# A search step's soundness flags: from a VectorE chain to eighteen GpSimd columns summed by TensorE

## The reference

```
for s in range(2):
    logits = (Xa @ W1) @ W2 @ (Xa @ W3).T
    # per row: keep the largest logits until their softmax mass reaches 0.9
    A  = softmax(where(keep, logits, -inf))
    Xf = Rf @ Xf;  Xb = Rb @ Xb;  Xa = A @ Xa
    Z  = Z + Xf @ U1[s] + Xb @ U2[s] + Xa @ U3[s]
out = x + layernorm(X + Z) * gamma + beta
```

## Time and profile before

| | us |
|---|---|
| median of 3 runs | 2169.99 (2163.16 to 2171.1) |
| profiled execution, its own time | 2169.9 |
| its span, first to last instruction | 2168.2 |

### The profile page before, as it was taken

The page is one execution under the profiler, slowest core; times in us unless marked ns, Lnnn a source line. Parts: engine busy times, 40 slices in busy tenths (PEclk is TensorE's granted clock), DMA queues, the critical chain, the costliest instruction groups (busy, mean ns, idle before and its releaser), DMA issues. The chain is left out here.

```text
span 2168.2 us, 32420 instructions
## 1 busy us (share of the span) xinstructions
PE 1883.3 (87%) x9866; PEld 1252.5 (58%) x9866; DVE 1912.8 (88%) x6117; ACT 1678.5 (77%) x1740; POOL 711.0 (33%) x1392
## 2 busy tenths in 40 slices
PE   3999765999999999999864999989998999999992
PEld 2566433666666666666642656565655566565662
DVE  7788889988899998889748899999999999999995
ACT  5444256999999999999626899989999898989840
POOL 2000043444334444434504333333333333333324
PEclk9999987999999999999986999999999999999996
DMA  7788330111111111111125010101010010101023
GB/s 262 295 317 312 114 130 20 34 56 55 51 55 55 35 54 55 51 55 56 34 75 207 1 45 23 45 23 45 23 36 32 24 44 23 45 23 45 22 94 121
DMA packets 65725, 167.61 MB, mean 77 GB/s; under 512 B 7037, under 2 KB 45307, under 8 KB 61947
## 3 DMA queue, kind: packets, MB, share of 16 engines
q1 hardware_dynamic: 65530, 165.43, 22.0%
HBM read 117.95 MB, written 47.45 MB: 76 GB/s over the span
## 5 line engine op out<-in xcount | busy, mean ns | idle before, releaser
L1468 PE MATMUL banks<-xa,pt 128*128 128x256 f32 x2704 | 644.2, 390 | 14.5 <-ACT pt L968 13.7
L1468 PEld LDWEIGHTS banks<-xa,pt 128*128 128x128 f32 x2704 | 507.0, 194 | 158.9 <-issue 71.3
L939 ACT ACTIVATE junk_a<-pb_all,minus_t 128x3327 f16<-128x3327 f32 x150 | 461.0, 3073 | 98.9 <-POOLq L862 96.4
L944 ACT ACTIVATE junk_a<-pb_all,minus_t 128x3327 f16<-128x3327 f32 x150 | 460.6, 3071 | 4.1
L1519 PE MATMUL banks<-region,at 128*128 128x512 f16 x2028 | 455.7, 380 | 0.0
L847 POOL TENSOR_SCALAR over<-over,points 128x1 f32<-128x1 f32 x150 | 97.1, 647 | 761.0 <-ACT junk_a L944 761.0
L1519 PEld LDWEIGHTS banks<-region,at 128*128 128x128 f16 x2028 | 196.4, 98 | 217.7 <-issue 1.3
L1394 PE MATMUL banks<-keys,qs 64*128 64x512 f32 (+1 forms) x816 | 190.1, 565 | 100.7 <-DMA qs<-q_d 31.0
L1260 DVE TENSOR_SCALAR_CACHE_REDUCE pb_all<-banks 128x1024 f32<-128x1024 f32 x260 | 209.2, 848 | 31.1 <-PE banks L1394 22.6
L1122 DVE MAX8 junk_v<-below 128x8 f32<-128x208 f32 (+1 forms) x624 | 222.4, 432 | 2.2
L968 ACT ACTIVATE pt<-banks 128x896 f32<-128x896 f32 x208 | 171.1, 859 | 63.6 <-PE banks L1460 63.4
(11 more groups left out here) (221 smaller groups left out, 2738.5 us busy)
## 6 DMA issues: line engine op xcount, KB each, us to landing
at<-adjT_d SPq DMA_DIRECT2D x52, 832.0 KB, 4.9
region<-in_adj_dram SPq DMA_DIRECT2D x25, 1663.5 KB, 7.9
adjT_d<-at SPq DMA_DIRECT2D x26, 832.0 KB, 3.9
fb_d<-fb_sb SPq DMA_DIRECT2D x26, 256.0 KB, 2.0
region<-fb_d SPq DMA_DIRECT2D x2, 3328.0 KB, 17.7
y_d<-y_sb SPq DMA_DIRECT2D x50, 128.0 KB, 1.7
x_d<-pb_all SPq DMA_DIRECT2D x1, 3328.0 KB, 10.4
qs<-q_d SPq DMA_DIRECT2D x104, 32.0 KB, 4.2
```

Of the source, the lines that this page charges most:

```text
L939: nc.scalar.activation(junk_a[:, 0:w], pb[u][:, 0:w], ACT.Relu, scale=sign, bias=t, accum_out=over[u][:, 0:1])\
L944: nc.scalar.activation(junk_a[:, 0:w], pb[u][:, 0:w], ACT.Sign, scale=sign, bias=t, accum_out=over[u][:, 1:2])\
L1468: last = nc.tensor.matmul(bank[4][:, 0:D], pt[sl][:, t * P:(t + 1) * P], xa[:, t0 + t, :], start=(t0 + t == 0), stop=(t0 + t == T - 1))
```

## The change

In step one only, VectorE no longer computes the flags. It signals `ranked` after the scan that makes `rank`. GpSimd gets a new function `flags(i)`, placed after level 0 of the tile two ahead and ahead of low_sub: it writes 18 columns, one for each segment and two for `took` and `left_max`, and signals `unsettled`. TensorE's first flag sum becomes a product of a column of ones with the 18 columns, and VectorE's `answer` takes the maximum of the 18 sums. VectorE writes `rest` in place where it wrote `same` and `rank`, because GpSimd still reads these.

```
...
                def flags(i):
                    by_segment = [v[:, 0:8 * G].rearrange("p (g e) -> p g e", e=8)[:, :, 7] for v in (cand, same, rank)]
                    pool.wait_ge(S("ranked"), i.t + 1)
                    after(pool, "any_psum", i, per=LOOKS)
                    ch.add(nc.gpsimd.tensor_scalar(signs_of[:, G:G + 1], took[:, :], 0.0, None, ALU.is_le))
                    ch.add(nc.gpsimd.tensor_scalar(signs_of[:, G + 1:G + 2], left_max[:, :], 0.0, None, ALU.is_le))
                    ch.add(nc.gpsimd.tensor_scalar(signs_of[:, 0:G], by_segment[2], ties[:, :], None, ALU.is_lt))
                    ch.link(nc.gpsimd.tensor_scalar(full[:, 0:G], by_segment[0], left_max[:, :], None, ALU.is_gt))
                    ch.link(nc.gpsimd.tensor_tensor(signs_of[:, 0:G], signs_of[:, 0:G], by_segment[1], ALU.mult))
                    ch.link(nc.gpsimd.tensor_tensor(signs_of[:, 0:G], signs_of[:, 0:G], full[:, 0:G], ALU.add))
                    pool.sem_inc(S("unsettled"), 1)
...
                        level(m, 0)
                        if i.inside(T):
+                            flags(i)
                             p = pb[i.third]
                             pool.wait_ge(S("low_removed"), i.t + 1)
...
-                    nc.vector.tensor_scalar(none[:, :], took[:, :], 0.0, None, ALU.is_le)
...
-                    nc.vector.tensor_scalar(none[:, :], left_max[:, :], 0.0, none[:, :], ALU.is_le, ALU.max)
...
-                        nc.vector.scalar_tensor_tensor(out=full[:, 0:G], in0=by_segment[2], scalar=ties[:, :], in1=by_segment[1],
+                        dve.sem_inc(S("ranked"), 1)
...
-                        nc.vector.scalar_tensor_tensor(out=full[:, 0:G], in0=by_segment[0], scalar=left_max[:, :], in1=full[:, 0:G],
...
-                        nc.vector.tensor_reduce(flaw[:, :], full[:, 0:G], AX.X, ALU.max)
...
-                        ch.link(nc.vector.tensor_tensor(unsettled[:, :], none[:, :], flaw[:, :], ALU.max), hold=True)
-                    dve.sem_inc(S("unsettled"), 1)
...
+                    if n == 1 and not first:
+                        nc.vector.tensor_reduce(any_un[0:1, 0:1], bank[0][0:1, LOOKS:LOOKS + G + 2], AX.X, ALU.max).then_inc(S("any_un"), 1)
...
+                    if n == 0 and not first:
+                        nc.tensor.matmul(bank[0][0:1, LOOKS:LOOKS + G + 2], ones8[:, 0:1], signs_of[:, :], start=True, stop=True)\
```

More of the change, by code:

```diff
@@ L226, in gnn_program @@
     none = sb("none", [P, 1], f32)
+    signs_of = sb("signs_of", [P, GMAX + 2], f32)
     any_un = sb("any_un", [P, LOOKS], f32)
@@ L1146, in search @@
                                                            op0=ALU.is_ge, op1=ALU.mult))
-                    nc.vector.tensor_scalar(none[:, :], took[:, :], 0.0, None, ALU.is_le)
+                    if first:
+                        nc.vector.tensor_scalar(none[:, :], took[:, :], 0.0, None, ALU.is_le)
                     nc.vector.tensor_tensor(run9[:, 0:1], run[:, 0:1], took[:, :], ALU.add)
@@ L1151, in search @@
                     nc.vector.reciprocal(rkept[i.slot][:, :], run9[:, 0:1])
-                    nc.vector.tensor_scalar(none[:, :], left_max[:, :], 0.0, none[:, :], ALU.is_le, ALU.max)
+                    if first:
+                        nc.vector.tensor_scalar(none[:, :], left_max[:, :], 0.0, none[:, :], ALU.is_le, ALU.max)
                     tied = nc.vector.scalar_tensor_tensor(out=rest[:, 0:R], in0=taken[:, 0:R], scalar=left_max[:, :], in1=ones_r[:, 0:R],
@@ L1160, in search @@
                         ch.link(nc.vector.tensor_tensor_scan(rank[:, 0:C], ones_r[:, 0:C], same[:, 0:C], 0.0, ALU.mult, ALU.add))
-                        nc.vector.scalar_tensor_tensor(out=full[:, 0:G], in0=by_segment[2], scalar=ties[:, :], in1=by_segment[1],
-                                                       op0=ALU.is_lt, op1=ALU.mult)
+                        dve.sem_inc(S("ranked"), 1)
                         ch.link(nc.vector.scalar_tensor_tensor(out=rest[:, 0:C], in0=rank[:, 0:C], scalar=ties[:, :], in1=same[:, 0:C],
                                                                op0=ALU.is_le, op1=ALU.mult))
-                        nc.vector.scalar_tensor_tensor(out=full[:, 0:G], in0=by_segment[0], scalar=left_max[:, :], in1=full[:, 0:G],
-                                                       op0=ALU.is_gt, op1=ALU.max)
-                        ch.link(nc.vector.scalar_tensor_tensor(out=same[:, 0:C], in0=q, scalar=left_max[:, :], in1=rest[:, 0:C],
+                        ch.link(nc.vector.scalar_tensor_tensor(out=rest[:, 0:C], in0=q, scalar=left_max[:, :], in1=rest[:, 0:C],
                                                                op0=ALU.is_gt, op1=ALU.max))
-                        nc.vector.tensor_reduce(flaw[:, :], full[:, 0:G], AX.X, ALU.max)
-                        ch.link(nc.vector.tensor_tensor(rank[:, 0:C], same[:, 0:C], q, ALU.mult))
-                    after(dve, "any_psum", i, per=LOOKS)
+                        ch.link(nc.vector.tensor_tensor(rest[:, 0:C], rest[:, 0:C], q, ALU.mult), hold=True)
                     if first:
+                        after(dve, "any_psum", i, per=LOOKS)
                         ch.link(nc.vector.tensor_tensor(unsettled[:, :], flaw[:, :], ties[:, :], ALU.max))
-                    else:
-                        ch.link(nc.vector.tensor_tensor(unsettled[:, :], none[:, :], flaw[:, :], ALU.max), hold=True)
-                    dve.sem_inc(S("unsettled"), 1)
+                        dve.sem_inc(S("unsettled"), 1)
                     if first:
@@ L1182, in search @@
                             d = below[:, g * W8:(g + 1) * W8]
-                            removed = nc.vector.match_replace(d, rank[:, 8 * g:8 * g + 8], d, 0.0)
+                            removed = nc.vector.match_replace(d, rest[:, 8 * g:8 * g + 8], d, 0.0)
                             if g == POOL_SEGMENTS - 1:
@@ L1214, in answer @@
                     dve.wait_ge(S("any_psum"), LOOKS * i.n + n)
-                    nc.vector.tensor_copy(any_un[0:1, n - 1:n], bank[0][0:1, n - 1:n]).then_inc(S("any_un"), 1)
+                    if n == 1 and not first:
+                        nc.vector.tensor_reduce(any_un[0:1, 0:1], bank[0][0:1, LOOKS:LOOKS + G + 2], AX.X, ALU.max).then_inc(S("any_un"), 1)
+                    else:
+                        nc.vector.tensor_copy(any_un[0:1, n - 1:n], bank[0][0:1, n - 1:n]).then_inc(S("any_un"), 1)
                 def look(i, n):
@@ L1413, in count_flags @@
                     pe.wait_ge(S("unsettled"), LOOKS * i.n + n + 1)
-                    nc.tensor.matmul(bank[0][0:1, n:n + 1], unsettled[:, :], ones8[:, 0:1], start=True, stop=True)\
-                        .then_inc(S("any_psum"), 1)
+                    if n == 0 and not first:
+                        nc.tensor.matmul(bank[0][0:1, LOOKS:LOOKS + G + 2], ones8[:, 0:1], signs_of[:, :], start=True, stop=True)\
+                            .then_inc(S("any_psum"), 1)
+                    else:
+                        nc.tensor.matmul(bank[0][0:1, n:n + 1], unsettled[:, :], ones8[:, 0:1], start=True, stop=True)\
+                            .then_inc(S("any_psum"), 1)
                 def turn_own(k):
```

## The result

The changed kernel takes 2200.45 us (2192.31 to 2211.26, four runs) against 2170.55: a ratio of 1.0154, 95% interval 1.0115 to 1.0192. The profiled execution spans 2209.5 us, 41.3 more than before. The sign was right and the size was not: 30 us where 102 were forecast.

A forecast was written before the change was run, and what follows sets the result against it. No single engine bounds the kernel, but a loop of waits between tiles, 36.97 us each. L939 at 12.05 plus 29.55 makes 41.6, +4.6 over 22 tiles is +102; 2169.9 + 102 = 2272 us, range 2240 to 2305.

The forecast's parts named there:

- Place of the flags: On GpSimd behind level 0: six operations and hand-over cost 2.08 us, flags ready at 1520.84, TensorE asking at 1517.95.
- TensorE's stall: At the first flag sum, TensorE waits from 1517.95 to about 1520.9; transposes start 1.25 us late after 1.70 of slack.
- VectorE's saving eaten by low_sub: On VectorE: 0.85 us saved a tile is lost because subtraction L1190 must wait for GpSimd's low_sub to end at 1523.3.
- The search ahead of the transposes: Between VectorE and TensorE: the search starts 0.5 us ahead of the finished tile's transposes instead of 0.57 behind.
- What that swing triggers: GpSimd's level 2 falls under VectorE's second pass L1117, delaying ScalarE's L939 to S + 12.05; every tile 41.6 us.
- T0: Start on TensorE of the transposes of the tile just finished; 1525.76 in the tile read, forecast to move by +1.25.
- S: Start of a search on VectorE; 1526.33 in the tile read, forecast to move by +0.2.
- The price of a held tile: Whole loop: ScalarE's L939 at S + 12.05 plus 29.55 to the next search gives 41.6 us against 36.97, +4.6.
- Rival (a): Level 2 slips out before L1117, only TensorE's wait costs: 38.2 us a tile, +1.24, total 2197 us; chance 0.10.
- Rival (b): Flags ready by 1519.65 hide under TensorE's slack; 0.85 x 22 = 19 us come off, total 2151; chance 0.04.

The follow-up runs named there:

- the kernel without the flags: Kernel before without step one's six VectorE flag operations, TensorE summing a column of zeros instead; 2151.26 us, ratio 0.9921.
- the kernel with the six waited operations: Kernel before plus six GpSimd operations on constants behind level 0, TensorE's first flag sum waiting for them, VectorE's flags kept; 2238.62 us, ratio 1.0331.
- three operations waited for: Kernel before, TensorE's first flag sum also waiting for a GpSimd signal behind level 0 and three added linked operations; 2212.02 us, ratio 1.018.
- the wait behind level 0: Kernel before, TensorE's first flag sum also waiting for a GpSimd signal right behind level 0, no operation added; 2165.02 us, ratio 0.9997.

## Why the prediction was wrong, point by point

- **Place of the flags: right.** Behind level 0 they come late, at the forecast time: 2.03 us from level 0's end to TensorE's sum against 2.08.
- **TensorE's stall: right.** 2.76 for 2.9, and an undisturbed start of the transposes 0.82 later into the tile than before for the 1.25 forecast.
- **VectorE's saving eaten by low_sub: right.** The good tile is 36.96, as before, and the subtraction is held for 0.73. The saving itself is 0.77 for 0.85 (the kernel without the flags).
- **The search ahead of the transposes: right in sign,** 0.26 for 0.5.
- **"What that swing triggers" failed.** I took level 2 to run from T0 + 6.26 to T0 + 8.07 in every tile, and so every tile to be slow. Those offsets came from one tile, and TensorE's clock was low there. Busy time by stretch of the kernel before, around T0 = 1525.76:

```profile
1524.00:1528.00 4.00, 2.48 (x17) 2.40 (x18) 3.20 (x14) 3.88 (x9) 2.82 (x6) 0.77 0.02 6
1528.00:1530.00 2.00, 2.00 (x8) 1.75 (x7) 1.90 (x4) 1.43 (x4) 0.04 (x1) 0.61 0.00 0
```

The clock was low behind T0 in eight of the 22 tiles of the earlier trace rows; I had read one of these. In the tile ahead of it, T0 is 1488.80 and the search starts at 1489.37. The clock is full there, and level 2 (timeline, GpSimd) is asked for at T0 + 5.54, 0.7 earlier:

```profile
1487.00:1491.00 4.00, 1.96 (x18) 1.65 (x18) 3.20 (x14) 3.88 (x10) 2.81 (x6) 1.00 0.01 2
```

```profile
1494.34 1.09 POOL L847 TENSOR_SCALAR over<-over,rough_t 128x1 f32<-128x1 f32 x1 [3.30 <-ACT junk_a L944]
...
1496.63 0.22 POOL L861 TENSOR_SCALAR minus_t<-points 128x1 f32<-128x1 f32 x1
```

Its first operation is held by the first pass, and the level ends at S + 7.48 all the same. That hold gives the level slack: it may be asked for later by some tenths and still end ahead of L1117. In the changed kernel the level is asked for at T0 + 5.2 in every tile from the second on. In the good tile with S = 1578.09 and T0 = 1578.35 (timelines, GpSimd and VectorE):

```profile
1583.55 0.61 POOL L848 TENSOR_SCALAR over<-over,rough_t 128x1 f32<-128x1 f32 x1 [3.76 <-ACT junk_a L959]
...
1585.37 0.22 POOL L862 TENSOR_SCALAR minus_t<-points 128x1 f32<-128x1 f32 x1
```

```profile
1585.82 3.69 DVE L1132 SCALAR_TENSOR_TENSOR below<-pb_all,cur 128x3327 f32<-128x3327 f32 x1
```

The level ends at S + 7.50, 0.23 ahead of the second pass; by my offset it would have ended at S + 8.33, under it. A swing of 0.8 us is inside the slack; one of 0.8 + 1.3, with the half clock, is not.
- **The price of a held tile was near:** 4.6 us over a good one forecast, 6.0 measured. ScalarE's sum starts where I put it (S + 12.05; 11.93 to 12.35 measured, once 13.05). What my sum lacks is a wait behind it. In each of the seven slow tiles ScalarE waits 0.37 to 1.84 us (1.1 in the mean) for VectorE's row maximum, and in no good one. In the tile from 1615.05 VectorE had itself waited 3.61 and 2.62 us for TensorE's logits, and TensorE's granted clock from 1634 to 1640 was 0.53; how much of the wait that clock makes is not shown. Timeline, ScalarE:

```profile
1643.36 3.07 ACT L936 ACTIVATE pb_all<-pb_all,negmax 128x3327 f32<-128x3327 f32 x1 [1.43 <-DVE negmax L1279]
```

The number of such tiles was wrong: 7 of 21, not all. That alone carries the miss: the forecast of 102 is 22 x 4.6, and the profiled execution shows 7 x 6.0.
- **Rival (a), TensorE's wait alone, 2197 us,** names nearly the measured time but not the way: no tile took its 38.2. The agreement is chance.
- **Rival (b), that it turns faster once the flags are ready in TensorE's slack,** named the condition. Moving the flags ahead of level 0 meets it and gives 2151, the figure worked out for it.
- I had the clock only as a mark in the profile (below 0.98; it was 0.96). It was the link that decides which tiles are slow.

What stays open: why some stalls of 2.76 us are followed by the half clock in the changed kernel and some not, while in the kernel with the six waited operations the stall at the end of every good tile was.

## What to carry to other kernels

A small operation moved to an idle engine lands behind whatever that engine has queued: compare when its turn comes with when its consumer asks, before counting what it saves. TensorE's stall in mid-work cost more than its length here, so a consumer on TensorE should ask late or be fed early: one call moved ahead of one level turned +1.5% into -0.7%. And offsets for a steady loop should be taken from several tiles, with the granted clock read beside each.

## What the runs showed of the hardware

- GpSimd and VectorE hold each other in both directions. VectorE's two-input subtraction, issued while GpSimd's two-input subtraction ran, took 3.27 us instead of 2.54; GpSimd's one-column operation under VectorE's pass took 3.59 instead of 0.27. The Trainium skill, "SBUF — State Buffer", section "Who interferes with whom", says that a VectorE instruction with two SBUF inputs contends with a GpSimd instruction that reads SBUF, that the port pair they share is an exclusive lock, and that the order of issue decides who blocks. Both numbers agree: the held operation ended 0.13 us behind the pass that held it (1626.59 and 1626.46), and the subtraction took 0.15 less than its own 2.54 plus the overlap of 0.88.
- TensorE standing idle for 2.6 to 3.05 us within continuous work was followed by 1.2 GHz in 8 of 16 cases in the changed kernel, from the second tile on. The 13 matmuls behind it then took 4.3 to 4.7 us (once 5.73) instead of 2.98. Stalls of 2.3 us were followed by it in 8 of 15 cases (three operations waited for), and stalls of 1.6 us (changed kernel) and of 1.0 us (the wait behind level 0) in none. The same delay filled with matmuls was followed by none: the granted clock over 22 tiles was 1.00 there, against 0.96 in the changed kernel. Where this idle stretch could not be removed, filling it with useless matmuls was worth 34 us, for 2.75 us of them a tile.
